# A two-stage graph network on one core: the bias of the node table moves to VectorE, and the first product of each quarter of edges moves ahead of the sums

## What is computed

```python
x = layernorm(x + relu(segment_sum(w * x[dst], src) @ W0.T))      # layer 0
npj = relu(layer_norm(x @ Wp + bp) * gp + betap)                  # 20 numbers a node
kron = relu(layer_norm(outer(npj[src], npj[dst]) @ Wk + bk) ...)  # 400 -> 256, per edge
kron_feat = segment_sum(kron, dst)
logits = relu(concat(x[dst], x[src]) @ We + be)                   # per edge
a = softmax of logits over the edges of each dst
hv = x @ Wn + bn
context = relu(segment_sum(hv[src] * a, dst))
# then a gated unit, two layer norms and a last linear layer per node
x = layernorm(x + result)
```

## Time and profile before

| | us |
|---|---|
| median of 3 runs | 9202.79 |
| lowest, highest | 9187.38, 9215.1 |
| the profiled execution: its time | 9201.89 |
| the profiled execution: its span | 9200.4 |
| node stage, about | 3960 to 4720 of the span |
| edge loop, about | 4720 to 8490 of the span |

### The profile page before, as it was taken

The page is one execution under the profiler, slowest core; times in us unless marked ns, Lnnn a source line. Parts: engine busy times, 40 slices in busy tenths (PEclk is TensorE's granted clock), DMA queues, the critical chain, the costliest instruction groups (busy, mean ns, idle before and its releaser), DMA issues.

```text
span 9200.4 us, 169831 instructions
## 1 busy us (share of the span) xinstructions
PE 6627.9 (72%) x32823; PEld 4195.6 (46%) x32824; DVE 5809.9 (63%) x16380; ACT 3779.0 (41%) x10923; POOL 4407.1 (48%) x4743
## 2 busy tenths in 40 slices
PE   3253666666666799988877777777777777777898
PEld 2122444444444577733334444444444444444444
DVE  8895444444443566644447777777777777776666
ACT  0000444444444100023336666666666666665333
POOL 0001777777778200000037776776666766674100
PEclk9676777777777999965569999999999999999988
DMA  0002333333322588844467777777777777776200
GB/s 12 0 0 79 100 100 99 99 101 99 99 97 96 194 262 263 262 186 197 192 208 210 205 205 203 204 203 205 200 205 199 207 202 204 203 204 175 64 19 18
DMA packets 973127, 1398.89 MB, mean 152 GB/s; under 512 B 378559, under 2 KB 744498, under 8 KB 959902
## 3 DMA queue, kind: packets, MB, share of 16 engines
q1 hardware_dynamic: 761663, 797.51, 29.0%
q0 software_dynamic: 208448, 596.38, 22.9%
q10 hardware_dynamic: 2586, 1.37, 0.1%
HBM read 986.18 MB, written 415.51 MB: 152 GB/s over the span
## 4 chain that ended last, share of the span: by engine, by line
PE 32%; issue 18%; DVE 16%; DMA 13%; SPq 8%; ACT 7%; POOL 3%; DVEq 1%; ACTq 1%; POOLq 0%
DMA arena_n<-rec_dram 8%; PE ps L1993 7%; SPq L550 7%; PE ps L1890 4%; PE ps L1787 4%; ACT junk L1001 3%; DMA arena_e<-msg_dram 3%; PE ps L2011 3%; PE ps L2002 3%; POOL msg_dram L814 2%; PE ps L1905 2%; DVE arena_r L1305 2%; DVE arena_e L1636 2%; DVE arena_e L1576 2%; ACT L1022 1%
## 5 line engine op out<-in xcount | busy, mean ns | idle before, releaser
L835 POOL DMA_INDIRECT arena_n<-tab_dram,idxs x2624 | 2621.1, 999 | 2756.0 <-DVE idxs L1551 1667.7
L1993 PE MATMUL ps<-arena_n 126*128 126x257 f32 x5232 | 1635.3, 416 | 404.6 <-DVE arena_e L1576 370.3
L814 POOL DMA_INDIRECT msg_dram<-arena_e,idxq x1616 | 1625.6, 1006 | 434.4 <-issue 424.9
L1001 ACT ACTIVATE junk<-ps 128x256 f32<-128x256 f32 x2616 | 995.2, 382 | 1065.8 <-PE ps L1993 937.5
L1879 PE MATMUL ps<-arena_n,arena_r 128*128 x3232 | 1085.1, 494 | 352.9 <-ACT arena_r L902 352.9
L1993 PEld LDWEIGHTS ps<-arena_n 126*128 126x128 f32 x5232 | 868.9, 196 | 910.1 <-DVE arena_e L1576 735.4
L1576 DVE COPY arena_e<-ps 128x257 f32<-128x257 f32 x1962 | 816.5, 422 | 681.7 <-ACT junk L1001 672.9
L1636 DVE SCALAR_TENSOR_TENSOR arena_e<-arena_e,rstd,nbetak_b 128x256 f32<-128x256 f32 x2608 | 1087.4, 481 | 31.6 <-ACT arena_e L1008 18.9
L1879 PEld LDWEIGHTS ps<-arena_n,arena_r 128*128 128x128 f32 x3232 | 753.6, 245 | 592.6 <-issue 466.2
L907 ACT ACTIVATE arena_e<-ps,recq 128x256 f32<-128x256 f32 x1616 | 736.7, 474 | 651.9 <-PE ps L1879 645.7
L1890 PE MATMUL ps<-arena_e,oh 128*128 128x256 f32 x3520 | 816.2, 387 | 88.8 <-DVE oh L1359 88.3
(11 more groups left out here) (335 smaller groups left out, 9115.5 us busy)
## 6 DMA issues: line engine op xcount, KB each, us to landing
arena_n<-m_dram SPq DMA_DIRECT2D x2624, 126.5 KB
arena_e<-msg_dram SPq DMA_DIRECT2D x441, 514.0 KB, 4.5
m_dram<-arena_e SPq DMA_DIRECT2D x49, 1413.5 KB, 4.9
m_dram<-arena_e SPq DMA_DIRECT2D x49, 1285.0 KB, 4.5
arena_n<-tab_dram,idxs POOLq DMA_INDIRECT x2624
hist_dram<-arena_r SPq DMA_DIRECT2D x163, 253.0 KB
arena_n<-rec_dram SPq DMA_DIRECT2D x1616, 2.0 KB
msg_dram<-arena_e,idxq POOLq DMA_INDIRECT x1616
```

Source lines behind the costliest of these rows:

```text
L814: nc.gpsimd.indirect_dma_start(out=msg_dram, in_=msgs[:, u, j, :], in_offset=None, out_offset=bass.IndirectOffsetOnAxis(ap=idxq[:, u, j:j ...
L835: nc.gpsimd.indirect_dma_start(out=feat[:, u, i, :], out_offset=None, in_=tab_dram, in_offset=bass.IndirectOffsetOnAxis(ap=idxs[:, u, i:i ...
L1001: nc.scalar.activation(junk[:, i % 2, 0:D], ps[:, bank_of(i), 1:HC], ACT.Square, scale=1.0 / 16, accum_out=var[:, u % 2, i:i + 1]).then_in ...
L1993: mm(ps[:, bank_of(i), 0:HC], prods_t[0:KM, s % 2, j * P:(j + 1) * P], m_ring[0:KM, i, :], start=True, stop=True).then_inc(e_h, 1)
```

## The change

Four things are changed. The bias row `wt_b` is loaded to all 128 partitions instead of one. TensorE no longer multiplies ones by it. ScalarE no longer copies the table row; VectorE adds bank and bias into `row` instead, right before it takes the statistics of the 20 numbers. And in the edge loop `linear(., 0)` and `square(., 0)` of a quarter move to the step in front: on TensorE behind `linear(main, 3)` and ahead of `softmax_products`, on ScalarE behind `square(main, 3)` and ahead of `copied(main)`.

```diff
-        wt_b = sb("wt_b", [1, ROW])
+        wt_b = sb("wt_b", [P, ROW])
...
-            act.dma_start(wt_b[:, 0:D], io[L1 + "bn"].unsqueeze(0)).then_inc(s_wt, 16)
+            act.dma_start(wt_b[:, 0:D], io[L1 + "bn"].partition_broadcast(P)).then_inc(s_wt, 16)
...
-            def table_rows(t):
-                act.wait_ge(n_tab, t + 1)
-                if not is_zero(t):
-                    act.wait_ge(n_st, 16 * t)
-                nc.scalar.activation(row, ps[:, 3, 0:ROW], ACT.Copy).then_inc(n_hv, 1)
...
-                if t is not None:
-                    table_rows(t)
...
                     if main is None:
                         if turned is not None:
                             evacuate(turned)
+                            square(turned, 0)
                         continue
                     g, u, s = main
                     one, two = earlier(it, main, 1), earlier(it, main, 2)
-                    square(main, 0)
-                    if turned is not None:
-                        evacuate(turned)
+                    evacuate(turned)
                     square(main, 1)
...
                     square(main, 3)
+                    square(turned, 0)
                     copied(main)
...
+            def table_row(t):
+                dve.wait_ge(n_tab, t + 1)
+                if not is_zero(t):
+                    dve.wait_ge(n_st, 16 * t)
+                tt(row, ps[:, 3, 0:ROW], wt_b[:, :], ALU.add).then_inc(n_hv, 1)
+
             def pj_stats(t):
+                table_row(t)
                 dve.wait_ge(n_hv, t + 1)
...
-                mm(ps[:, 3, 0:ROW], ones[0:1, :], wt_b[:, :], start=True, stop=False)
                 for c in range(2):
                     ins = mm(ps[:, 3, 0:ROW], tr2[:, 1, c * P:(c + 1) * P], wt[:, c, :],
-                             start=False, stop=(c == 1))
+                             start=(c == 0), stop=(c == 1))
...
                     if main is not None:
-                        linear(main, 0)
                         linear(main, 1)
                     if turned is not None:
                         turn_products(turned)
...
                         linear(main, 2)
                         linear(main, 3)
+                    if turned is not None:
+                        linear(turned, 0)
+                    if main is not None:
                         softmax_products(it, main)
```

More of the change, by code:

```diff
@@ L867, in _ @@
             act.dma_start(bk_b[:, :], io[L1 + "bk"].partition_broadcast(P)).then_inc(s_wt, 16)
-            act.dma_start(wt_b[:, 0:D], io[L1 + "bn"].unsqueeze(0)).then_inc(s_wt, 16)
-            act.dma_start(wt_b[:, D:D + 1], io[L1 + "be"].unsqueeze(0)).then_inc(s_wt, 16)
-            act.dma_start(wt_b[:, PS0:PS0 + K], io[L1 + "bp"].unsqueeze(0)).then_inc(s_wt, 16)
+            act.dma_start(wt_b[:, 0:D], io[L1 + "bn"].partition_broadcast(P)).then_inc(s_wt, 16)
+            act.dma_start(wt_b[:, D:D + 1], io[L1 + "be"].partition_broadcast(P)).then_inc(s_wt, 16)
+            act.dma_start(wt_b[:, PS0:PS0 + K], io[L1 + "bp"].partition_broadcast(P)).then_inc(s_wt, 16)
             act.dma_start(gk_b[:, :], io[L1 + "gk"].partition_broadcast(P)).then_inc(s_wt, 16)
```

## The result

On the chip of the forecast (called the first chip in what follows) the changed kernel takes 8941.21 us (median of 4 runs, 8936.67 to 8948.64) against 9202.03 us of the kernel before (4 runs, 9187.38 to 9215.1): ratio 0.9718, 95% interval 0.9701 to 0.9735. The forecast was 9005 us with a range of 8950 to 9090.

The account below looks back on a forecast made before the run. The prediction took TensorE's work in each tile's chain to bound the node stage, and a ring of waits, no single engine, the edge loop. 9201.9 - 58.6 - 139 = 9004 us, forecast as 9005, range 8950 to 9090.

Parts of the forecast that it names:

- The node term: Node stage: without the bias product the chain is 1.22 us a tile shorter in 48 of 49 tiles, 58.6 us.
- The cover for VectorE's add: Node stage: VectorE's new 0.44 us add fits before M part 5 with 0.75 us left, so it costs nothing.
- a change of level in the node stage's clock: Node stage: TensorE's clock changing level was listed as a sign that the prediction is wrong; no size given.
- The edge term: Edge loop: moving one product and one square saves 3.47 us a pass, 139 us over 40 passes.
- Steps 0 and 1: Edge loop, first two steps of a group: the moved product fills TensorE's idle time, 0.45 us each, 0.89 taken together.
- Steps 2 and 3: Edge loop, last two steps of a group: no new gain, 0 each; the earlier 0.89 us is carried.
- The jump: Edge loop, the group with the loop's jump, once a pass: 0.8 us gained, ends 0.37 and 1.95 us.
- The rival of the clock that stays up: Edge loop: TensorE's clock no longer falls at the loop's jump, 46 us more gain, 8959 us; chance 0.14.
- VectorE did not take over: Edge loop: VectorE becomes the limit after the first gain, the second 0.45 us is lost, 9074 us; chance 0.17.
- GpSimd hardly bound: Edge loop: GpSimd's gathers, about 20.65 us a group, are next behind the forecast 20.83 us but do not bind.
- The slower case: Edge loop: ScalarE's early square blocks its queue, 0.57 us a step, 365 us lost, 9401 us; chance 0.05.
- The product that holds up the sums: Edge loop: the moved product waits for a copy and holds the sum behind it; second 0.45 us lost, chance 0.17.

Follow-up runs that it names:

- row_by_dve: Kernel before with the bias product kept and the node's row copied out of PSUM by VectorE instead of ScalarE: ratio 1.0009.
- bias_128: Kernel before with the bias product over all 128 rows, rows 1 to 127 zero: 11264.51 us against 11359.95, ratio 0.9922.
- the node part alone: Kernel before with bias loaded to 128 partitions, no bias product, row added by VectorE, edge loop in old order: 11099.37 us against 11189.67, ratio 0.9934.

## Why the prediction was wrong in size

**The node term, 58.6 us forecast, 90.6 measured: mis-sized.** The step read "the bias product is gone: 1.22 us a tile, directly in the chain". The cover for VectorE's add held: it starts at 4304.81, takes 0.45 us for the forecast 0.44, and M part 5 still waits for TensorE (0.64 us, forecast 0.75). ScalarE's copy was off the path, as `row_by_dve` shows. What failed is that a product was priced by its own duration, in one tile read for all. Per ordinary tile (15.56 to 13.65): 1.22 us for the product, 0.30 for the weight load of the products behind it, which it had left in the open, and 0.39 because the M parts now run partly at 2.4 GHz (2.10 to 1.71): 1.91 us, 90 us in 47 tiles. The load and the clock, 0.69 us a tile, had no term in the sum. `bias_128` shows that both are the row count's doing and not the product's presence. The hint stood in the rows: the earlier trace rows have a mean clock of 0.52, hardly above the lower level, and the tile of the earlier trace rows has its M parts partly at 2.4 GHz, so it could not stand for the stage. The prediction named a change of level in the node stage's clock as what would make it wrong, and gave it no price.

**The edge term, 139 us forecast, 175.4 measured.** By its steps:

- Steps 0 and 1, 0.45 us each: measured 0.44 and 0.52. Right, idle and waits as described.
- Steps 2 and 3, 0 each: measured a loss of 0.09 and a gain of 0.11. An ordinary group wins 0.98 us instead of 0.89.
- The fourth group of a pass was 22.02 us long and not 21.72; I had read only the one in the middle, and took it for all three. All three are 20.73 to 20.75 us long now, so the fourth wins 1.28 us by its median. In it ScalarE's copy came 1.00 us behind the start of the turns, in the middle group 0.72 (6414.61 behind 6413.89), with nothing in the trace that it could have waited for. The fourth group of before:

```profile
6435.63 0.60 PE L1787 MATMUL ps<-ident,arena_n 128*126 128x128 f32 x4
...
6436.63 0.60 ACT L991 ACTIVATE arena_n<-ps 126x512 f32<-126x512 f32 x1 [0.76 <-PE ps L1787]
```

- The jump, 0.8 us: 0.96 by the mean of 40 groups (25.76 to 24.80). The gap itself is shorter than I assumed, 3.5 us on average, and in 9 of 39 passes the clock was at 1.00 behind it, in 3 of the 31 looked at before. The rival of the clock that stays up came true in part: 23% of the jumps against 10%.

Together 4.33 us a pass by the mean of 40 passes (91.31 to 86.98) instead of 3.47. The groups' spread is gone as well: four hiccups of about 1.4 us in groups of before have no match after.

**The rivals.** VectorE did not take over. GpSimd hardly bound: the chain of waits goes through its gathers for 62 us of 3500 in the edge loop. But it is occupied nearly all of the time: 64 gathers of 1.046 us on average and as many gaps of 0.30 make 86.1 us of a pass of 87.0. The median gather takes 0.946 us, as before, and the longest 2.03; if the long ones wait for something, GpSimd's own limit is nearer to 80 us (64 x 1.25), and no run shows which. The slower case was priced on ScalarE's square; the runs show that on chips where the change does lose, it is TensorE's order that loses. The product that holds up the sums was named in the forecast, but its price was only that half of a gain is lost, never that the loop gets longer.

**The range** was too narrow on its good side: both terms were summed from rows of one tile and one group, and neither end allowed for what a removed product does to its neighbours and to the clock.

## What to carry to other kernels

A TensorE product costs more than its row in the chain: ask what the products on either side become without it, and when the clock rises. Of the three ways to add the bias measured here the product of one row is the dearest; padded to 128 rows with zeros it cost as little as the add on VectorE, and that is a smaller edit.

A gain that is made of filled idle time in a ring of waits holds for the conditions in which the idle time was measured. Time both orders on a second chip before keeping one: of the kernels here the node part alone (0.9934) or `bias_128` (0.9922) is best on the later chips, and the whole change won 2.8% on the first, where the others were not timed.

When one tile or one group of a loop is read for all, read its siblings first: the tile picked here was not an ordinary one, which the mean clock of the stage could have told, and the group picked did not stand for the fourth of a pass.

## What the hardware did that I had not expected

- The same kernel took 9202 us in one series and 11158 to 11360 us in all those of three later chips; on one of these it took 11360 and, later, 11160. The node stage was the same to 1% (733 and 731 to 734 us), the edge loop 40 to 45% longer (3730 against 5235 to 5403 us), and what lies ahead of the node stage 460 to 520 us longer. ScalarE's and VectorE's instructions took as long as before; TensorE's were longer, at a granted clock of 0.74 to 0.82 in the edge loop instead of 0.98.
- On those chips SyncE's small instructions last from 2 ns to 1.4 us (the register moves of its loads: median 29 ns), those of the other engines hardly vary.
- A weight load started together with its product, and not 0.43 us ahead of it, where a product of one row stood next to products of 128 rows: 0.3 us on either side, in every tile.
- With the product of one row TensorE's clock rose in 8 of 49 tiles, and 10.6 us behind the first transpose; with the same product over 128 rows it rose in 47, 7.8 us behind it.
